# A decoder layer on one core: the query weight folded into the context keys once, and the work regrouped into three independent threads

## The reference, cut to what matters

```
x = x + self_attention(layernorm(x))          # 16 heads of 16, rotary, causal
x = x + cross_attention(layernorm(x), ctx)    # 16 heads of 64, 77 context rows
x = x + ffn(layernorm(x))                     # 256 -> 1024 -> 256, exact gelu

# cross attention, per head h
Q = LN(x) @ W_Q[:, h]        # 256 x 64
K = ctx @ W_K[:, h]          # 77 x 64
V = ctx @ W_V[:, h]          # 77 x 64
scores = where(mask, -1e9, Q @ K.T / 8)
out    = softmax(scores) @ V            # then all heads @ W_O
```

## Time and profile before

| | |
|---|---|
| median of 3 runs | 650.27 us (647.83 to 650.78) |
| profiled execution, span | 650.2 us |
| PE busy | 545.2 us (84%), 4526 matmuls |
| DVE / ACT / POOL busy | 394.7 / 296.8 / 192.5 us |
| mean granted TensorE clock | 0.914 |
| residual of self-attention done (L1644), element 0, 1, 7 | starts at 90.28, 172.16, 575.04 us |

### The profile page before, as it was taken

One profiled execution on the slowest core, in us unless ns is written; L12 is line 12 of the kernel. 1 busy time (PEld: TensorE's weight loads), 2 busy tenths in 40 slices (PEclk: granted clock), 3 DMA queues, 4 the chain that ended last, 5 costly groups with the idle time before them and its releaser, 6 DMA issues.

```text
span 650.2 us, 11972 instructions
## 1 busy us (share of the span) xinstructions
PE 545.2 (84%) x4526; PEld 457.3 (70%) x4526; DVE 394.7 (61%) x1121; ACT 296.8 (46%) x450; POOL 192.5 (30%) x284
## 2 busy tenths in 40 slices
PE   4678876888898799979997999899989898988846
PEld 3665565665887598758975897679767776686736
DVE  4577265973678538954895379637962596255432
ACT  3334441335634465447445634474546444643313
POOL 3525431307242324232423232143223111411110
PEclk9799898975999989989999799899997999698858
DMA  8593573034030412124212412051115100100000
GB/s 279 170 284 116 209 178 55 1 114 113 3 114 2 92 49 85 32 56 84 71 46 58 82 49 66 18 124 49 51 27 115 33 1 5 41 17 1 1 0 17
DMA packets 47161, 47.28 MB, mean 73 GB/s; under 512 B 14672, under 2 KB 42976, under 8 KB 47104
## 3 DMA queue, kind: packets, MB, share of 16 engines
q1 hardware_dynamic: 45600, 41.57, 24.7%
q0 software_dynamic: 1504, 4.95, 2.1%
HBM read 30.71 MB, written 15.53 MB: 71 GB/s over the span
## 4 chain that ended last, share of the span: by engine, by line
PE 59%; DVE 17%; issue 7%; ACT 6%; POOL 5%; DMA 3%; SPq 3%; DVEq 0%; ACTq 0%; POOLq 0%
PE banks L626 11%; PE banks L628 10%; PE banks L627 9%; PE banks L924 5%; PE banks L868 5%; PE banks L879 5%; DVE banks L1609 4%; PE banks L782 3%; DMA k_stack<-rot_dram 2%; PE banks L768 2%; DVE c_lo L1565 2%; POOL work L509 2%; PE banks L821 1%; PE banks L745 1%; PE banks L851 1%
## 5 line engine op out<-in xcount | busy, mean ns | idle before, releaser
L1609 DVE CUSTOM_DVE_ANT_0 banks<-banks,causal_qk 128x256 f32<-128x256 f32 (+1 forms) x256 | 83.9, 386 | 8.9 <-PE banks L745 8.9
L509 POOL TENSOR_TENSOR work<-work,rc 128x616 f32<-128x616 f32 x32 | 38.9, 1216 | 142.3 <-DVE rc L1698 142.3
L520 POOL TENSOR_SCALAR_AFFINE_SELECT probs<-probs 128x256 f32<-128x256 f32 x128 | 50.9, 425 | 89.4 <-ACT probs L1240 89.4
L1207 ACT ACTIVATE work<-banks 77x1024 f32<-77x1024 f32 x32 | 32.7, 1020 | 77.5 <-PE banks L868 77.5
L1240 ACT ACTIVATE probs<-banks 128x768 f32<-128x768 f32 x64 | 50.6, 811 | 29.8 <-PE banks L768 25.2
L626 PE MATMUL banks<-k_hi,q_hi 128*128 128x256 f32 (+1 forms) x160 | 54.6, 342 | 4.8 <-DVE k_lo L1482 4.8
L1565 DVE TENSOR_TENSOR q_lo<-work,q_hi 128x512 fp32r<-128x512 f32 x32 | 21.9, 688 | 47.3 <-ACT q_hi L1207 47.3
L868 PE MATMUL banks<-ident,work 128*77 128x128 f32 x256 | 37.7, 295 | 14.5 <-DVE c_lo L1565 8.1
L626 PE MATMUL banks<-wo_hi,c_hi 128*128 128x256 f32 x128 | 41.5, 324 | 7.8 <-DVE c_lo L1565 7.8
L627 PE MATMUL banks<-k_lo,q_hi 128*128 128x256 f32 (+1 forms) x160 | 47.7, 298 | 0.0
L628 PE MATMUL banks<-k_hi,q_lo 128*128 128x256 f32 (+1 forms) x160 | 47.4, 296 | 0.0
(11 more groups left out here) (180 smaller groups left out, 1730.2 us busy)
## 6 DMA issues: line engine op xcount, KB each, us to landing
rot_dram<-rot_s_hi SPq DMA_DIRECT2D x16, 256.0 KB, 2.1
rot_dram<-rot_s_lo SPq DMA_DIRECT2D x16, 256.0 KB, 2.1
q_stack<-rot_dram SPq DMA_DIRECT2D x32, 128.0 KB, 4.0
k_stack<-rot_dram SPq DMA_DIRECT2D x32, 128.0 KB, 4.0
k_raw<-k_dram SPq DMA_DIRECT2D x16, 154.0 KB, 3.3
v<-v_dram SPq DMA_DIRECT2D x8, 308.0 KB
x_in<-in_x SPq DMA_DIRECT2D x8, 256.0 KB, 3.1
q_stack<-rot_dram SPq DMA_DIRECT2D x32, 64.0 KB, 3.9
```

The lines of the kernel that those rows point to most:

```text
L509: pool.tensor_tensor(sc2[g % 2], sc2[g % 2], rc2[:, g % 2].rearrange("p g a -> p g a ()").broadcast_to([P, 4, 2, S2]), ALU.mult).then_inc( ...
L520: last = pool.affine_select(out=diagonal, in_=diagonal, compare_op=ALU.is_ge, fill=0.0, base=0, pattern=[[0, 2], [1, P]], channel_multipli ...
L1207: act.activation(dst, src, ACT.Copy).then_inc(done, 1)
L1609: last = dve.tensor_tensor_reduce(out=held[:, at], in0=held[:, at], in1=bias, scale=-1.0, scalar=HUGE, op0=ALU.add, op1=ALU.min, accum_out ...
```

## The change

Four things are changed together.

1. **Fold.** `queries`, its splits (`q2`) and the per-element key loads are gone. In the setup `keys(m, half)` now splits its result into two pieces in SBUF (`kT`), and `fold_keys(m, k, half)` multiplies the turned query weight by them, 6 matmuls of 64 contraction rows and 308 columns each, in pairs on rows 0 to 63 and 64 to 127. ACT empties banks 5 and 6, DVE banks 3 and 4, into a staging buffer (two of them), and SP stores that to `fold_dram`, 16 DMAs of 631 KB in runs of 616 bytes. Per element and group SP loads 315 KB back (`load_fold`), ACT and POOL split it (`fold_hi`, `fold_lo`), and `scores2` multiplies LN(x) with it directly: 12 matmuls of 308 columns a group, 12 of 256 before.
2. **Own buffers.** f gets its own norm, transpose and split buffers (`xn_f`, `xfT`), x1 is doubled, hidden activations have their own tile.
3. **Own banks.** Self-attention has banks 0 to 2, cross attention 3 to 6, FFN bank 7 and, for every second group of `hidden`, bank 5. `shifted` has one pair of banks in place of two; `transpose2` goes through bank 5 in two halves, with two copies by ACT.
4. **New order.** The loops are gone; every engine's list is written out for all 8 elements. While self-attention of element i runs, cross attention is at i-1 and FFN at i-2. Loads of W_proj and W_O of the cross attention wait for the end of the fold, whose buffers they use.

The core of the diff:

```diff
-            def queries(b, g):
...
-                for c in range(2):
-                    m = 2 * g + c
-                    for k in range(KD):
-                        mm = product(halves(3 + g)[:, c, :], both(wq2, slice(None), k, slice(m * P, (m + 1) * P)),
-                                     both(xbT, slice(None), k), k == 0, k == KD - 1)
-                mm.then_inc(q2_ps, 1)
+            def fold_keys(m, k, half):
+
+                u = (m * KD + k) * 2 + half
+                pe.wait_ge(kx_lo, 2 * m + half + 1)
+                if u == 0:
+                    pe.wait_ge(w_lo[WQ_W], 1)
+                if u >= 2:
+                    pe.wait_ge(fold_ok[u % 2], u // 2)
+                at = 5 - 2 * (u % 2)
+                cols = slice(half * HS, (half + 1) * HS)
+                for w, x_ in ((0, 0), (0, 1), (1, 0)):
+                    for p in range(2):
+                        rows = slice(64 * p, 64 * p + DX)
+                        mm = pe.matmul(bank[:, at + p, 0:HS], wq_turned[w][rows, m, k * P:(k + 1) * P],
+                                       kT[m % 2][x_][rows, cols], start=(w == 0 and x_ == 0), stop=(w == 1))
+                mm.then_inc(fold_ps, 1)
...
+            def store_fold(m):
+                sp.wait_ge(fold_ok[0], 2 * m + 2)
+                sp.wait_ge(fold_ok[1], 2 * m + 2)
+                g, c = divmod(m, 2)
+                for k in range(KD):
+                    sp.dma_start(fold_dram[:, g, k, :, c * 2 * S2:(c + 1) * 2 * S2].rearrange("b p n -> p b n"),
+                                 stage[m % 2][:, k].rearrange("p b a s -> p b (a s)")).then_inc(fold_st[m % 2], 16)
...
+                pe.wait_ge(g_lo, 4 * b + g + 1)
+                for q in range(QT):
+                    dst = bank[:, 3 + q, 0:GW]
+                    pe.matmul(dst, ident_bf[:], mask_bf[:, q, 0:S2].rearrange("p s -> p () s").broadcast_to([P, GH, S2]),
+                              start=True, stop=False)
+                    for k in range(KD):
+                        mm = product(dst, both(xbT, slice(None), k, slice(q * P, (q + 1) * P)),
+                                     both(fold, slice(None), k, g), False, k == KD - 1)
+                mm.then_inc(s2_ps, 1)
...
-                bk, back = shifted_bank(a, g)
-                if g >= back and (a == 0 or g != 3):
-                    pe.wait_ge(p_ok, HH * a + g + 1 - back)
+                if g > 0:
+                    pe.wait_ge(p_ok, HH * a + g)
...
+            keys(1, 1)
+            fold_keys(1, 0, 0)
+            scores(0, 0, 2)
+            fold_keys(1, 0, 1)
```

More of the change, by code:

```diff
@@ L222, in decoder_layer, with hidden_bank @@
         MAX_BANKS = (1, 2)
[L224 to L244, removed]
+        def hidden_bank(g):
+            return 7 - 2 * (g % 2)
         STACK_DMAS = 16
@@ L441, in drain @@
-            def drain(b):
-                pass
-            elements(first, step, drain)(sp)
+            first_input()
+            weight(QKV_W)
+            weight(WK_W)
+            trig_tables()
+            load_x(1)
+            weight(CTX_W)
+            weight(WQ_W)
+            store_rotated(0)
+            weight(WV_W)
+            stacks(0, 0)
+            stacks(0, 1)
+            residual_input(0)
+            weight(WO_W)
+            store_fold(0)
+            store_fold(1)
+            store_fold(2)
@@ new lines, in _ @@
+            keys(6, 0)
+            keys(6, 1)
+            scores(0, 7, 2)
+            fold_keys(6, 0, 0)
+            fold_keys(6, 0, 1)
+            fold_keys(6, 1, 0)
+            fold_keys(6, 1, 1)
+            keys(7, 0)
+            keys(7, 1)
+            fold_keys(7, 0, 0)
+            fold_keys(7, 0, 1)
+            fold_keys(7, 1, 0)
+            fold_keys(7, 1, 1)
+            transpose_max(0, 1)
+            shifted(0, 0)
+            shifted(0, 1)
+            values2(0, 0)
+            values2(0, 1)
@@ new lines, in _ @@
+            hidden(1, 2)
+            scores(3, 2, 5)
+            scores2(2, 0)
+            hidden(1, 3)
+            project_down(1, 0)
+            scores(3, 3, 5)
+            scores2(2, 1)
+            scores(3, 4, 5)
+            project_down(1, 1)
+            transpose2(2, 0, 0)
+            transpose_max(3, 0)
+            scores(3, 5, 5)
+            transpose2(2, 0, 1)
+            scores(3, 6, 5)
+            weigh2(2, 0)
+            scores2(2, 2)
+            transpose2(2, 1, 0)
@@ new lines, in _ @@
+            transpose_b(6)
+            hidden(5, 3)
+            scores(7, 3, 8)
+            scores2(6, 0)
+            scores(7, 4, 8)
+            project_down(5, 0)
+            project_down(5, 1)
+            transpose_max(7, 0)
+            scores(7, 5, 8)
+            scores2(6, 1)
+            transpose2(6, 0, 0)
+            scores(7, 6, 8)
+            transpose2(6, 0, 1)
+            scores(7, 7, 8)
+            weigh2(6, 0)
+            scores2(6, 2)
+            transpose2(6, 1, 0)
@@ new lines, in _ @@
+            keys(6, 1)
+            fold_keys(6, 0)
+            fold_keys(6, 1)
+            keys(7, 0)
+            keys(7, 1)
+            fold_keys(7, 0)
+            fold_keys(7, 1)
+            split_hi(WV_W)
+            maxima(0, 1)
+            exponentials(0, 0, 2)
+            exponentials(0, 1, 2)
+            values2(0, 0)
+            values2(0, 1)
+            values2(1, 0)
+            values2(1, 1)
+            exponentials(0, 2, 2)
+            exponentials(0, 3, 2)
+            values2(2, 0)
@@ L1948, in _ @@
-            elements(first, step, drain)(dve)
-IN_ORDER = ["x", "ctxT", "mask", "wqT", "wkT", "wvT", "woT", "wQ", "wK", "wV", "wO", "wfcT", "bfc", "Afc", "BfcT",
+            statistics_a(0)
+            norm_a(0)
+            split_lo(QKV_W)
+            xaT_part(0)
+            rotary(0, 0)
+            rotary(0, 1)
+            statistics_a(1)
+            split_lo(WK_W)
+            split_lo(CTX_W)
+            norm_a(1)
+            split_lo(WQ_W)
+            keys(0, 0)
+            xaT_part(1)
```

2874 lines of the change are left out of this document (1896 added, 978 removed).

## The result

The changed kernel takes 656.9 us (median of 16 runs, 650.1 to 663.6), the kernel before 649.8 in the same session: a ratio of 1.0123, 95% interval 1.0082 to 1.0163. It is slower by 1.2%, where 622 was forecast (594 to 656). Ratios leave out the runs that lie over 1.5% above the fastest one of their kernel; medians keep them. The profiled execution has a span of 649.0 at a mean granted clock of 0.924, while the other runs go from 648.4 (0.927) to 661.9 (0.908).

A forecast was written before the change was run, and what follows sets the result against it. The prediction took PE, busy 84% of the span, to bound the repeated steps, while both ends wait. Setup 135 + first gap 60.7 + six gaps 355.8 + tail 71 = 622.5, stated as 622; range for 8 in 10, 594 to 656.

The forecast's parts named there:

- I take half of the idle time as recovered: 59.3 a gap.: Six gaps between self-attention residuals: the new order recovers half of PE's 6.0 us idle, 59.3 each, 355.8 in all.
- So a gap falls by 4.75 if its idle time stays.: Each of the six gaps: PE's net saving from dropping queries takes 67.15 to 62.4 us, the upper end.
- The setup, 135: Start to self-attention's residual of element 0: `shifted` starts at 100, then 35 us more; 135, up 44.7 from 90.3.
- my warm end (6.9): Fold in the setup: 6.9 us per query block at full clock, against 9.3 cold; 8.8 was taken.
- the 4 us of switches: Fold in the setup: some 40 switches between half-height and full-height matmuls at 0.10 us, at most 4 us more.
- The slow fold as a rival: Setup: stores of 616 bytes or DVE's list make 12.5 us a block, residual at 161, total 648; chance 0.12.
- The attention thread as the bound (gaps of 66): Six gaps: the attention thread's chain plus cross attention's DVE share keeps them near 66, total 669; chance 0.13.
- PE idle over 8: Profile sign for the attention thread as bound: gaps above 63.9, PE idle over 8 us, ended by exponentials or maxima.
- First gap and tail: Residual of element 0 to 1, 81.9 to 60.7 us; after element 7's residual, 75.2 to 71 us.
- The clock: Setup's fold stage alternates work and waits: throttled 9.3 us a block, warm clock 6.9.
- the stage runs cold: Fold in the setup: by the skill's throttled default state, 9.3 us a block.
- The break-even gap of 63.9: Six gaps: above 63.9 us each, with setup 135, first gap 60.7 and tail 71, the fold is not paid back.

The follow-up runs named there:

- b_query1: Kernel before, with one of the six matmuls of each query tile (40 of 48 per element left out): 637.3 us, ratio 0.9810.
- a_halfstore: Changed kernel, storing only the fold parts of elements 0 to 3, which elements 4 to 7 read again: 653.1 us, ratio 1.0113 to the kernel before.
- a_max: Changed kernel, with self-attention's maxima for the second query tile taken over the diagonal block of 128 keys alone: 648.6 us, 0.9989 to the kernel before.
- a_fold1: Changed kernel, with one of three products in the context's keys and in the fold: 650.3 us, ratio 1.0075 to the kernel before.
- a_down1: Changed kernel, with one of the three products of `project_down` (32 of 48 matmuls per element left out): 654.5 us, 1.0099 to the kernel before.
- a_order_late: Changed kernel, same instructions, the five lists in another order from about 190 us on: 640.1 us, ratio 0.9920 to the kernel before.
- a_order_mid: Changed kernel, same instructions, lists reordered from about 100 us on with table loads priced; the best order found: 630.7 us, 0.9729 to the kernel before.

## Why the prediction was wrong, step by step

- **"I take half of the idle time as recovered: 59.3 a gap."** This is the term of the sum that failed. None of the idle time was recovered: PE is idle 7.6 us a gap and was 6.9, and the gap is 62.45, which makes 18.9 of the 26.5 us. What was open was how well the five lists were laid: with the same instructions in another order the gap is 59.7 and PE idle for 5.5, so the order held the missing part and not the design.
- **"So a gap falls by 4.75 if its idle time stays."** The step under it failed as well, though its 62.4 is what was measured; that is luck. PE's busy share was taken for its being the bound, and the idle time does not stay: with 4.9 us of query matmuls left out, it rises by 2.6 and the gap falls by 1.9 (`b_query1`), and 31 us of other matmuls are worth 1 to 3 us in all, in three orders. The other 2.8 us (67.15 - 1.9 - 62.45) came with everything else that was changed. No run separates the three threads and their buffers from the query copies and subtractions that went, which were priced at nothing, though DVE stood 18.0 us for ACT at these subtractions. The Trainium skill (Perfetto Trace Analysis, Identifying the Most-Contended Engine) would have PE's headroom judged by its MFU (the share of peak FLOP/s) and the busy share of its weight loads, and the engine with the highest occupancy worked on first. The share of the weight loads was 70%, still the highest, so by this figure the rule names PE too, and the runs do not bear it out for this kernel.
- **The setup, 135.** Right by two errors that cancel, which is luck. The fold runs from 33.95 to 88.42, 6.8 us a block, my warm end (6.9), not 8.8. I had PE at work for under half of it, and it was busy for 43.9 of 54 us; the 4 us of switches cannot be seen in the block. But `shifted` to residual took 47.3 and not 35. PE's rows there show a part of it:

```profile
88.42 0.50 PE L939 MATMUL banks<-q_stack,k_stack 50*128 50x128 f32 x4
90.38 0.80 PE L939 MATMUL banks<-q_stack,k_stack 50*128 50x128 f32 x4 [1.46 <-ACT probs L1731]
91.47 0.79 PE L781 MATMUL banks<-wfc_hi,fold_hi 128*128 128x512 f32 x1 [0.30 <-DVE wfc_lo L2237]
...
98.25 0.49 PE L939 MATMUL banks<-q_stack,k_stack 50*128 50x128 f32 x4
```

  After two waits the context's values begin at the 1.2 GHz level (0.43 us a matmul for the first twelve, where 0.24 was counted), and three groups of them stand between two `shifted`. The clock of that stretch is 0.70. The rest of the 12 us isn't broken down.
- **The slow fold as a rival.** Wrong, and `a_halfstore` shows that stores were no part of it.
- **The attention thread as the bound (gaps of 66).** Nearer than its 0.13, as `a_max` shows, but not met as it was put: its sign, PE idle over 8, did not come, and of DVE's three longest waits two are for cross attention's chain (`c_lo` 37.2 us from 200 to 560) and one of 8.9 is for the store of a result, ready at 387.8 and issued by POOL at 437.1, because its place in POOL's list is late:

```profile
DVE c_lo L2320 <- ACT c_hi L1699: 37.2, 19, 8.5
DVE sm L2462 <- ACT work L1763: 10.5, 10, 2.1
DVE work L2483 <- DMA out_y<-work: 8.9, 1, 8.9
```

- **First gap and tail** were 4.3 and 2.6 us too low, and stayed so in the best order: for these it isn't shown what holds them.
- **The clock** was weighed for the setup alone. From 34 to 88 the fold had 0.86, so "the stage runs cold" did not come; with less work it had 0.56. The Trainium skill (TensorE: Matmul & The Clock Gate, What's actually happening) calls the throttled state the default that activity releases. Both figures agree with that; what failed was my reading of this stage as a throttled one.
- **The break-even gap of 63.9** rested on 60.7 and 71 for the first gap and the tail. With the measured setup, 65.0 and 73.6 it is (650.2 - 135.7 - 65.0 - 73.6) / 6 = 62.65, and the gap of 62.45 lies just under it, as the span does (649.0 against 650.2). By the medians the changed kernel is slower. The kernel before was profiled at its median clock (0.914, 0.915) and the changed one above its own (0.924, 0.917), which goes the right way; that it is the whole difference isn't shown.

## What to carry to other kernels

An engine that is busy 84% of the time is the bound only if less work on it shortens the span. Ask that of the chip before a change is built on it: leave out a few microseconds per step of its work and see what comes back. Where lists of fixed order carry several threads, the order is worth as much as the change (26 us here, against 1 to 12 us for 31 to 39 us of matmuls), and it has to be laid with the prices that the trace shows, table loads among them. The 2.7% by which the best order lies under the kernel before compare new lists that were laid anew with old ones that were not; whether the old design would gain as much is open.

## What the runs showed of the hardware

- Where matmuls were left out, the granted clock of those that stayed was lower: 0.86 to 0.56 in one stretch (`a_fold1`), 0.917 to 0.890 over the whole (`a_down1`).
- The same lists were granted different clocks from one execution to the next: 0.83, 0.85 and 0.97 from 34 to 84 us (`a_order_late`, the changed kernel, `a_order_mid`), with the end of the fold at 89.5, 88.4 and 84.0.
- A table load on ACT takes 1.28 us, and an order that sets GELU among exponentials took 12 more of them, 15.4 us of ACT.
- DMA engines that were busy 94% of 54 us were not what PE waited for: with half of the stores left out (busy 44%) the date after them moved by 1.6 us (`a_halfstore`).
